# Moving three pieces of vector-engine work in a four-layer mixture-of-experts kernel: routing in two sets, a split ahead of weight turns, weight turns two slots later

## What is computed

```python
x = x + L0_ffn(L0_cond(x))      # cond: 8 gelu experts, top 2 of sigmoid(router) + a shared silu part
                                # ffn: 8 relu-squared experts, top 2 of sigmoid scores
x = x + L1_ffn(L1_cond(x))      # cond: GRU over the 128 steps; ffn: 8 gelu experts of width 512, softmax of top 2
x = x + L2_ffn(L2_cond(x))      # cond: low-rank term, gelu; ffn: as layer 1
x = x + L3_ffn(L3_cond(x))      # cond: tanh RNN over the 128 steps
# L3_ffn: top 3 of 12, two mixtures:  h = gelu(sum_e dw1[:, e] * (x @ W1[e].T));  y = sum_e dw2[:, e] * (h @ W2[e].T) + dw3 @ b2
```

## Time and profile before

| | |
|---|---|
| device time, median of 3 runs | 635.3 us (634.16 to 636.39) |
| the profiled execution: time / span of its instructions | 633.13 us / 631.4 us |
| PE busy | 607.3 us, 96% of the span |
| DVE busy | 345.0 us, 55% |
| ACT busy | 286.9 us, 45% |
| POOL busy | 110.4 us, 17% |
| mean granted clock of PE | 0.998 of full speed |
| chain of work that ended last | PE 78%, DVE 14%, ACT 3%, issue 3%, DMA 1% |

### The profile page before, as it was taken

How to read it: one execution, slowest core, us unless ns; L and a number is a source line. 1 busy time by engine, 2 the same in 40 slices (tenths; PEclk the granted TensorE clock), 3 DMA queues, 4 the chain that set the end, 5 groups by cost and what they waited for, 6 DMA issues and landing times.

```text
span 631.4 us, 12504 instructions
## 1 busy us (share of the span) xinstructions
PE 607.3 (96%) x4574; PEld 564.7 (89%) x4574; DVE 345.0 (55%) x1205; ACT 286.9 (45%) x955; POOL 110.4 (17%) x325
## 2 busy tenths in 40 slices
PE   8889999999999999999999999998999999999996
PEld 7678788889999999999999999998989889898895
DVE  4875656754464454445554553158747664765514
ACT  3275645645655455444554456545823323311110
POOL 3134111111111111111111110000211221321310
PEclk9999999999999999999999999999999999999999
DMA  8998000000000000000000000091102002002000
GB/s 259 342 300 126 1 1 2 2 2 1 2 2 1 2 1 2 2 2 1 3 1 2 1 2 2 24 178 31 72 2 69 37 5 103 5 6 100 9 1 8
DMA packets 47309, 26.94 MB, mean 43 GB/s; under 512 B 28340, under 2 KB 42512, under 8 KB 46736
## 3 DMA queue, kind: packets, MB, share of 16 engines
q1 hardware_dynamic: 45224, 25.66, 15.1%
q10 hardware_dynamic: 2024, 0.48, 0.4%
HBM read 25.57 MB, written 0.57 MB: 41 GB/s over the span
## 4 chain that ended last, share of the span: by engine, by line
PE 78%; DVE 14%; ACT 3%; issue 3%; DMA 1%; SPq 0%; POOL 0%; DVEq 0%; POOLq 0%
PE Y L1364 30%; PE U L1364 27%; PE HH L1364 7%; PE ZR L1364 7%; PE M L1364 6%; DVE acc_a L803 3%; DVE gated L795 1%; DMA l_bc<-dw 1%; ACT gated L637 1%; DVE rank L835 1%; DVE acc_b L803 1%; DVE rh L803 1%; DVE relu L795 1%; DVE cmp_a L795 0%; DVE fresh L803 0%
## 5 line engine op out<-in xcount | busy, mean ns | idle before, releaser
L1364 PE MATMUL Y<-l_dn,gated 128*128 128x128 f32 x1152 | 162.9, 284 | 1.4 <-DVE acc_a L803 0.7
L1364 PEld LDWEIGHTS Y<-l_dn,gated 128*128 128x128 f32 x1152 | 141.1, 192 | 4.6 <-issue 3.2
L637 ACT ACTIVATE gated<-U,b1T 128x256 f32<-128x256 f32 x256 | 106.6, 473 | 0.0
L1364 PE MATMUL U<-l_x_hi,l_up_hi 128*128 128x256 f32 x256 | 82.8, 324 | 1.0 <-DVE l_x_lo L795 1.0
L619 ACT ACTIVATE h<-ZR,rnn_b 128x8 f32<-128x8 f32 x128 | 34.2, 267 | 95.1 <-PE ZR L1364 92.9
L803 DVE SCALAR_TENSOR_TENSOR fresh<-zr_s,cand 128x8 f32<-128x8 f32 x128 | 21.4, 167 | 95.0 <-ACT cand L615 92.7
L1364 PE MATMUL U<-l_x_lo,l_up_hi 128*128 128x256 f32 x256 | 72.0, 281 | 0.0
L1364 PE MATMUL U<-l_x_hi,l_up_lo 128*128 128x256 f32 x256 | 72.0, 281 | 0.0
L539 POOL TENSOR_SCALAR zh<-zr_s 128x8 f32<-128x8 f32 x128 | 25.7, 201 | 255.4 <-ACT zr_s L611 255.4
L615 ACT ACTIVATE cand<-HH 128x8 f32<-128x8 f32 x128 | 22.7, 177 | 96.3 <-PE HH L1364 96.3
L1364 PE MATMUL U<-scaled_hi,l_up_hi 128*128 128x256 f32 x192 | 58.1, 302 | 1.4 <-POOL scaled_lo L555 1.4
(11 more groups left out here) (263 smaller groups left out, 1207.7 us busy)
## 6 DMA issues: line engine op xcount, KB each, us to landing
l_bc<-dw SPq DMA_DIRECT2D x4, 1536.0 KB, 6.4
stage<-L_ffn_W_dram SPq DMA_DIRECT2D x4, 768.0 KB, 10.4
w_raw<-L_ffn_W_dram SPq DMA_DIRECT2D x12, 256.0 KB, 7.0
l_up_raw<-L_ffn_W_dram SPq DMA_DIRECT2D x1, 2048.0 KB, 9.6
l_up_raw<-L_ffn_w_dram SPq DMA_DIRECT2D x1, 2048.0 KB, 14.6
l0f_up<-L_ffn_w_dram SPq DMA_DIRECT2D x1, 768.0 KB, 7.2
l0f_dn<-L_ffn_w_dram SPq DMA_DIRECT2D x1, 768.0 KB, 8.7
x<-x_dram SPq DMA_DIRECT2D x1, 512.0 KB, 4.4
```

The lines of the kernel that those rows point to most:

```text
L637: last = nc.scalar.activation(gated[:, n % 4, h * N:(h + 1) * N], U[n % 2][:, h * N:(h + 1) * N], ACT.Gelu, bias=b1T[:, col:col + 1])
L1364: return nc.tensor.matmul(out, lhsT, rhs, start=start, stop=stop, skip_group_check=shared)
```

## The change

Five edits. (1) `route_c` takes tiles 2 and 3 in slots 4 to 9 and tiles 4 to 7 in slots 10 to 15, with the comparison tables of the second set in a buffer of layer 3. (2) Chunk 0's ffn routing also goes through `route_f_quarter`, and `route_f` goes. (3) `split_l1` stands directly behind the slot's GRU step. (4) `W2_SLOT` is two later: DVE turns piece e in slot 164 + e. (5) ACT's copy follows two slots behind the turn (its loop 166 + e) and the difference three behind it (slots 167 to 172).

```diff
-L3_ADDR, L3_SCORE, L3_DW, W2_SLOT = [C3 + CT // 2 + i for i in (0, 1, 9, 6)]
+L3_ADDR, L3_SCORE, L3_DW, W2_SLOT = [C3 + CT // 2 + i for i in (0, 1, 9, 8)]
...
-                if 0 <= n - W2_SLOT < E3:
-                    e = n - W2_SLOT
+                if 0 <= n - 1 - W2_SLOT < E3:
+                    e = n - 1 - W2_SLOT
                     sc.wait_ge(w2_turned, e + 1)
...
-            def route_c(tiles, parts):
+            def route_c(tiles, parts, room=(relu[:, 0, :], relu[:, 1, :])):
...
-                if 0 <= e - 2 < W2_LATE:
-                    w2_low(e - 2)
+                if 0 <= e - 3 < W2_LATE:
+                    w2_low(e - 3)
...
-                        if n < GRU_SLOT:
-                            route_f(n, (3,))
-                    if n >= GRU_SLOT:
-                        route_f_quarter(n, quarter)
+                    route_f_quarter(n, quarter)
                     if quarter == 2:
                         take_sums(n)
                     if n != 4:
                         add_l0(n - 3, quarter)
                     if quarter == 3 and REST_C <= n < REST_C + 6:
-                        route_c(range(TILES, GX), (n - REST_C,))
-                    if quarter == 3 and n < GRU_SLOT:
-                        route_f(n, (1, 2))
+                        route_c(range(TILES, 2 * TILES), (n - REST_C,))
+                    if quarter == 3 and REST_C + 6 <= n < REST_C + 12:
+                        route_c(range(2 * TILES, GX), (n - REST_C - 6,), (l3_cmp_a[:, 0:4 * E * E], l3_cmp_a[:, 4 * E * E:8 * E * E]))
...
             for n in range(A_START, SLOTS):
...
-                route_f(n)
...
                 for step in steps:
                     gru_update(step)
+                    split_l1(step)
                 take_sums(n)
...
                 l3_ahead(n)
-                for step in steps:
-                    split_l1(step)
```

More of the change, by code:

```diff
@@ L934, in route_c @@
                 sig_c, mask_c, gap_c, comb_c = sig_a[:, cols], mask[:, cols], gap[:, cols], comb_x[:, cols]
-                room = relu[:, 0, :], relu[:, 1, :]
                 if 0 in parts:
```

## The result

The changed kernel takes 636.4 us (median of 20 runs) against 633.9 for the kernel before in the same series: a ratio of 1.0036, 95% interval 1.0024 to 1.0048, so 2.3 us slower (1.5 to 3.0). It was forecast at 635.6 and "within 0.3%". It lies inside the range and 0.06% past that bound, on the slower side; the interval reaches to both sides of the bound. The forecast rested on 635.3 for the kernel before, the median of three runs, 1.4 us over that of the 20 here. As a difference it was +0.3 us, against 2.3 measured.

The account below looks back on a forecast made before the run. PE, busy 96%, was taken as the bound, with DVE edits mattering only where PE stands still. +2.1 - 1.0 - 1.8 + 1.0 = +0.3 us on 635.3 gave 635.6 us, range 632.5 to 638.2.

Parts of the forecast that it names:

- Edit 1, +2.1: Layer 0: second set puts 2.7 us of DVE work ahead of first F adds, less 0.6 gained: +2.1 us.
- Edit 2, 0: Layer 0, chunk 0's F routing: same work before the first F add, 0 us, bounds -0.2 and +0.4.
- edit 3, -1.0: Slot 139: the split ends before PE asks, so PE's 0.99 us wait goes, -1.0 us.
- Edits 4 and 5, -1.8: Slots 162 to 165: ACT's waits for the turn and PE's waits for the tanh go, -1.8 us, up to -2.3.
- The end, +1.0: Slots 170 to 175: 3.4 us more DVE work, mostly filling idle time, delays the last add: +1.0 us, bounds 0 and +3.4.
- the slower rival: Slots 170 to 176: DVE and POOL in turns, operations double, end +4.2, total +3.5, 638.8 us; chance 0.2.
- the rule: A DVE operation with two SBUF inputs and a GpSimd operation reading SBUF exclude each other for the whole instruction.
- The sum: Whole kernel: +2.1 - 1.0 - 1.8 + 1.0 = +0.3 us, 633.4 profiled, 635.6 at the median.
- a case that missed by 0.4 us: Whole kernel: stalls are traded, time within 0.3%, 633.4 to 637.2 us; chance 0.5.
- The signs: If right: DVE idle about 3 us before `l_in`, F adds at 43 to 44, slot 140 and turn waits gone.
- the signs of being wrong: F projections before 32 us, F adds on time, or layer 2's last add late with `l_dn_lo` rows near 1.3 us.
- The faster rival: Layer 0's second set costs PE nothing, the end 0.5: -2.3, 633.0 us, or 632.5 with the end free; chance 0.3.

Follow-up runs that it names:

- edit 1 alone: Only the two-set cond routing of layer 0 added to the kernel before: ratio 1.0050 [1.0030, 1.0070], +3.2 us.
- the whole change with `W2_LATE = 3`: The changed kernel with the W2 differences of pieces 3 to 5 left to layer 3: ratio 0.9997 against the kernel before, 633.4 us.
- the profile with the operations left out: Two-set routing alone on the kernel before, tiles 4 to 7 getting scores as weights in one copy, without ranking or normalization: ratio 0.9997, -0.2 us.
- edits 4 and 5 alone: Only the later W2 turns, with copy and difference behind them, on the kernel before: ratio 1.0003 [0.9979, 1.0027], +0.2 us.
- W2_LATE 6 against 3: W2 differences 3 to 5 in the slots against left to layer 3: changed kernel 636.4 against 633.4 us; moved W2 turns only, ratios 1.0003 against 0.9958.
- edit 3 alone: Only the split moved directly behind the GRU step, on the kernel before: ratio 0.9995 [0.9978, 1.0013], -0.3 us.
- `W2_LATE` = 3 alone: The kernel before with only the W2 differences of pieces 3 to 5 left to layer 3: ratio 1.0007 [0.9988, 1.0026], +0.4 us.
- whole change, copies first: Changed kernel, W2 differences 3 to 5 in layer 3, ACT's rounding of layer 1's first two weight pieces one slot later: ratio 0.9967, 632.2 us.

## Why the prediction came out as it did

**What bounds each stretch** was read right: apart from stretches at half clock, edits paid and cost where the stretches of the earlier trace rows and slot 140 show PE idle.

**Edit 1, +2.1**: the profile gives +2.5, within a scatter of 2.6, and edit 1 alone +3.2 (1.9 to 4.4). Right in its main term: the F adds came 1.75 us later (3.7 in edit 1 alone, where DVE left slot 9 0.5 us earlier, as forecast), the start of the F part gained 0.4 us at most, and without the second set's operations nothing was left of the cost. Two things weren't in it. The standstill of about 3 us ahead of `l_in`, foreseen as harmless, was followed by a stretch at half clock in both profiles that had it (31 to 39 us, edit 1 alone and the whole change with `W2_LATE = 3`), and taking the standstill away gave 1 to 2 us back. And in the whole change it was the last C adds, which edit 2 mixes with the F routing, and not the first F adds, that held PE. How the cost splits between the operations and that stretch stays open: the profile with the operations left out didn't have the standstill.

**Edit 2, 0**, and **edit 3, -1.0**: the first right by its own run (-0.2, -1.0 to +0.6), the second right in the two profiles (-1.0 between `silu` and `z1m`) and not decided by its run (-0.3, -1.4 to +0.8).

**Edits 4 and 5, -1.8**: -2.3, the upper bound given. Both waits went; that the other 0.5 us come from the copies that left ACT's queue was the prediction's reason and wasn't tested by itself.

**The end, +1.0: the term that was mis-sized, by a step that failed.** The prediction counted 3.4 us of DVE work into 5.35 us of idle time by the earlier trace rows and took "most can be filled". The profiles show +4.0 (whole change) and +3.9 (edits 4 and 5 alone), and 2.5 to 2.9 us of it went with three differences (W2_LATE 6 against 3, in two pairs of kernels). In its place stands the slower rival's mechanism, DVE and POOL in turns. It priced the end at +4.2 and the whole at 638.8. Its place and its mechanism were right, its list was not: of the differences one doubled, and the others were three `l_weighted` products pushed beside POOL. That its price came out so near was partly luck: of the 4.0 us up to 1.7 are the stretch at half clock, which it didn't have, and 2.5 are waits. It got 0.2, because only one wait of 1.50 spoke for it; the earlier trace rows with a median of 1.13 against a least of 0.69 were the rows that deserved the weight. One of the two rows that the prediction took as agreeing with the rule, `okay` at 32.53, has only one input, so it isn't the kind of operation that the rule was cited for. The Trainium skill (SBUF — State Buffer, SBUF's two separate sides) states the rule, an exclusive lock for the whole instruction in favour of the one that starts first; the rows at 449.43 and 449.99 agree, for POOL (1.78) as for DVE (1.76). With +4.2 in the place of +1.0 the sum would have been +3.5 in the profiled execution, where +3.1 was measured.

**The sum** was 0.3 where the profiled pair shows 3.1 and the runs 2.3. The pair shows more than the runs: the profiled execution of before was one of its faster ones, 0.8 us under the median of its 20 runs and without a half-clock stretch before its last microseconds. The total was near by luck: 635.6 against 636.4 looks like 0.8 us, but 1.4 us of too high a median for the kernel before stood against a difference taken 2 us too small. The chances had 0.5 on a case that missed by 0.4 us, less than the interval is wide, and 0.2 on the side that came.

**The signs** that it gave: seen were the missing waits in slot 140 and for `l_dn_turned`, the RNN waits under 0.5 us, bank waits of 2.3 us (3 forecast) and F adds at 42.92 (43 to 44). Not seen were the long idle time ahead of `l_in`, except in other kernels, and a stretch from slot 162 to layer 3 shorter by 1 us: from `z1m` to `l_in` it is 1.65 us longer. Of the signs of being wrong, one `l_dn_lo` row of 1.37 us came.

**The faster rival** fell at edit 1 (3.2 us, not 0) and at the end.

## What to carry to other kernels

Idle time on DVE isn't free to fill where POOL works from SBUF: ask of each operation with two SBUF inputs, and of a small one with a single input too, which POOL operation it will lie beside, and add up to that operation's whole duration (here up to 1.1 us), not a share. The place to look for room is where POOL is idle: three differences cost nothing measurable in slots 167 to 169 of the old order and 2.5 us a few slots on. And behind a wait that an edit leaves standing or makes longer, look at the clock: some waits here had a stretch at half clock behind them that cost up to as much again. Last, one profile of before is one execution: a wait like the 1.60 us ahead of `l_in` can be missing from the next.

## What the runs showed of the hardware that was not expected

**PE's clock falls to half for short stretches inside a busy program.** The prediction took it as 1.00 throughout, as the profile of before shows it. Every profile of an experiment shows one to four stretches at 1.2 instead of 2.4 GHz ahead of the last microseconds, most of about 3.4 or 6.8 us, and that of the changed kernel three. Several stand behind a wait of PE:

| kernel | PE's wait before it | stretch |
|---|---|---|
| changed | 1.88 us at 41.69 | 42 to 46 |
| changed | 2.17 us at 461.54 | 462 to 466 |
| edit 1 alone | 3.22 us up to 32.69 | 31 to 39, from within the wait |
| edits 4 and 5 alone | 2.18 us at 475.49 | 476 to 480 |
| edit 3 alone | the RNN waits of the earlier trace rows, 1.49 us | 436 to 444 |
| `W2_LATE` = 3 alone | the same, 1.49 us | 436 to 440 |
| whole change, copies first | 1.89 us at 40.44 | 41 to 46 |

Not every such wait has one: the wait of 2.27 us at 46.30 with edit 1 alone had none, nor had the 1.49 us of the earlier trace rows in the kernel before itself. And ten of the 14 profiles, that of the changed kernel among them, have one that begins between 11 and 13 us, in instructions that are the same in all; the kernel before has none there. A stretch in which PE has no gap costs about half its length: 6.8 us cost 3.1 in the second half of layer 2 with edit 3 alone, 3.4 us cost 1.5 with `W2_LATE` = 3 alone. Times and mean clocks go together: spans of 631.4 us at 0.998 and 634.5 at 0.988 for the two kernels compared here, and, among the runs of the kernel before alone that were timed beside the experiments, medians of 632.1 us at 0.999 (5 runs), 634.0 at 0.993 (26) and 636.1 at 0.988 (6). This is shown as a coincidence in time, and for the cause no run was made.

**A small DVE operation can cost as much as a large one.** Beside POOL's 1.27 us difference an operation of 32 columns took 1.29 us and one of 256 columns 1.37: what is added is the rest of POOL's operation, whatever the DVE operation's own size. An operation with one input can be hit too: `okay`, 6 columns, took 1.18 us in the earlier trace rows and ended with POOL's operation, and the same instruction on 2 columns took 0.16 in the changed kernel. The transposes of 0.70 us and the adds from PSUM of 0.3 us each kept their length beside POOL.
